# Sparse cross-attention: the scores of a later tile between the two halves of a tile's sums of values, and four columns of negated maxima

## The chip, the cores and the metric

One core of one Trainium2 chip runs the whole program. The metric is the device time in microseconds (us) of one execution; lower is better. TensorE is PE in the profile, VectorE is DVE, ScalarE is ACT, GpSimd is POOL and SyncE is SP. Each engine runs its own instructions strictly in the order in which the program gives them, and waits at semaphores for the others.

## The reference

The program is a four-layer perceiver on `x` [16, 64, 128] with a context of 16 x 1601 x 128. Each layer has a cross-attention, an attention and a feed-forward. The change lies in the cross-attention of the last layer, where each query keeps only its 32 highest of 1601 scores in each of 16 heads:

```python
Q = _split_heads(x @ Wq.T + bq, N_HEADS)
K = _split_heads(knowledge_embeddings @ Wk.T + bk, N_HEADS)
V = _split_heads(knowledge_embeddings @ Wv.T + bv, N_HEADS)
scores = jnp.einsum('bhsd,bhnd->bhsn', Q, K) / SCALE
k = min(TOP_K, N)                                   # 32
topk_scores, topk_indices = jax.lax.top_k(scores, k)
sparse_weights = jax.nn.softmax(topk_scores, axis=-1)
sel_V = jnp.take_along_axis(V[:, :, None, :, :], topk_indices[..., None], axis=3)
context = jnp.einsum('bhsk,bhskd->bhsd', sparse_weights, sel_V)
context = context.transpose(0, 2, 1, 3).reshape(B, S, D_MODEL)
return context @ Wo.T + bo
```

## The kernel before

The stages of the program follow one another. The change is in `topk_cross_attention` alone, which runs from about 2660 us to 4140 us of the span.

Its work is cut into T = 128 tiles. A tile is one batch and two of its 16 heads: 128 rows (2 heads x 64 queries) by 1601 keys. Eight tiles (TB = 8) make a batch. The kernel doesn't gather the 32 chosen values: it makes a dense 128 x 1601 matrix P that is zero outside the chosen scores, and multiplies P by the context. A tile goes through these steps, each named as in the code:

- `scores(t)` on PE (L925): four blocks of keys into psS, the one score buffer of four banks. It waits until `copy_scores(t-1)` and `fold(t-1)` have read the previous tile out of psS.
- `copy_scores(t)` on ACT (L1012): psS to SS, three buffers.
- `fold(t)` on DVE (L1162): the pairwise maxima of the two halves of a row. It reads psS and SS.
- `find` and `drop` on DVE (MAX8 at L1184, MATCH_REPLACE8 at L1193): the 32 highest, eight at a time. `find(t,0)`, `drop(t,0)`, `find(t,1)`, `drop(t,1)` belong to one turn of the loop, `find(t,2)`, `drop(t,2)`, `find(t,3)` to the next. `add_halves` (L1111) and `take_maxes` (L1118) on POOL prepare the pairwise minima for the later ones.
- `negate(t)` on DVE (L1200): the row's maximum times -1 into a column of `mneg`, which has two columns. Before it writes a column it waits for `exps(t-2)`, which read it.
- `exps(t)` on ACT (L1018): EX = exp(SS + mneg).
- `count_sides` (ACT, L1030), `count_above` (DVE, L1211), `count_equal` (three small steps on POOL, L1126 to L1132) and `mark` (ACT, L1039 and L1042) make P, a one for each chosen score; `weigh` on POOL (L1139) multiplies it by EX.
- `turn(t,q)`, q = 0 to 3, on PE (L935) transposes P in four groups of blocks into psT, and `copy_weights(t,q)` on ACT (L1050) copies each to PT. `values(t,q)` on PE (L947) multiplies each group by the context into psU: 4, 4, 4 and 1 products, each two instructions in the trace. So `values(t,0)` and `values(t,1)` are 16 rows, `values(t,2)` and `values(t,3)` are 10.
- `inverse(t)` on DVE (L1218), `norm(t)` on ACT (L1058), `turn_u(t)` on PE (L959) and `copy_ut(t)` on ACT (L1066) scale and transpose the result. After every 16 tiles a pair of batches is summed over the heads in four parts, `sums` (PE, L968) and `add` (DVE, L1225), each in a turn of its own.

Each engine runs one loop over s = 0, 1, 2, ... in which steps of different tiles stand beside one another. In turn s, ACT has: `count_sides(s-2)`, `copy_scores(s+1)`, `norm(s-4)`, `copy_weights(s-3, 0 and 1)`, `mark(s-2)`, `copy_weights(s-3, 2 and 3)`, `exps(s-1)`, `copy_ut(s-4)`. DVE has: `find(s,0)`, `find(s-1,2)`, `negate(s)`, `drop(s,0)`, `drop(s-1,2)`, `find(s,1)`, `inverse(s-4)`, `find(s-1,3)`, `drop(s,1)`, `add` in some turns, `fold(s+1)`, `count_above(s-1)`. POOL has: `take_maxes(s)`, `count_equal(s-2)`, `add_halves(s+1)`, `weigh(s-2)`, and once in eight turns `spread` (L1101), which spreads the next batch's queries. PE's order is the loop at L975, in the listing.

Three kinds of turns differ in length. In a key turn (t = s-3 is one of the first four tiles of a batch, in the first 15 batches) PE also projects a block of the next batch's keys (`project`, L914) and ACT copies it (`keys`, L1005). In a sum turn (28 of them: t mod 16 = 5, 6, 7 or 13, from t = 21 on) stand `sums` and `add`; `turn_u` waits for that `add`. All others are plain turns.

Of the kernel before, what the change touches and what calls it, by code (L numbers as in the profile page):

```python
# [5 lines left out]
ALU = mybir.AluOpType  # L6
ACT = mybir.ActivationFunctionType
# [9 lines left out]
K = 1601  # L17
# [10 lines left out]
ONE = 1  # L28
# [764 lines left out]
def topk_cross_attention(c, N, QT, WkT, bk):  # L793
# [4 lines left out]
    T = B * TB  # L798
# [7 lines left out]
    with ExitStack() as st:  # L806
# [4 lines left out]
        SS = c.sb(st, "SS", [128, 3, KP])  # L811
        maxes = c.sb(st, "maxes", [128, 2, HALF])
        pairs = c.sb(st, "pairs", [128, 3, KP])
        EX = c.sb(st, "EX", [128, 2, K])
        P = c.sb(st, "P", [128, 2, K])
        PT = c.sb(st, "PT", [128, 2, NC, 128])
        top = c.sb(st, "top", [128, 3, TOPK])
        mneg = c.sb(st, "mneg", [128, 2])
        above = c.sb(st, "above", [128, 2])
        below = c.sb(st, "below", [128, 2])  # L820
        sides = c.sb(st, "sides", [128, K])
# [29 lines left out]
        exp_done, marked = c.sem("exp_done"), c.sem("marked")  # L851
# [7 lines left out]
        with nc.Block() as block:  # L859
            @block.gpsimd  # L860
            def _(pool):
                for j in range(2):
                    pool.memset(ctxN[:, j, :, D:D + 1], 1.0).then_inc(filled, 1)
                for j in range(3):
                    pool.memset(SS[:, j, K:KP], LOW).then_inc(filled, 1)
                pool.tensor_tensor(c.x[:], c.x[:], bc(c.bias_row[:].rearrange("p (a d) -> p a d", a=1), [128, NT, D]),
                                   ALU.add).then_inc(filled, 1)
                pool.wait_ge(filled, 6 + ONE)

        with nc.Block() as block:  # L870
# [24 lines left out]
            @block.tensor  # L895
            def _(pe):
                def bank_free(use):
                    u = slot[use]
                    if u >= 2:
                        kind, a, n = uses[u - 2]  # L900
                        if kind == "keys":
                            pe.wait_ge(kt_ready, BLOCKS * a + n + 1 + ONE)
                        else:
                            pe.wait_ge(pt_ready, 4 * a + n + 1 + ONE)
                    return u % 2

                def project(b, n):
                    o, w = KB[n]
                    pe.wait_ge(turned_loaded[b % 2], 16 * (b // 2 + 1) + ONE)
                    if b == 0:  # L910
                        keys = psS[:, o:o + w]
                    else:
                        keys = psT[:, bank_free(("keys", b, n)), 0:w]
                    pe.matmul(keys, WkT, ctxT[:, b % 2, o:o + w], start=True, stop=True).then_inc(kp_ready, 1)  # L914

                def scores(t):
                    b, n = t // TB, t % TB
                    if n == 0:
                        pe.wait_ge(kt_ready, BLOCKS * (b + 1) + ONE)
                        pe.wait_ge(stat_ready, b + 1 + ONE)  # L920
                    if t:
                        pe.wait_ge(copied, t + ONE)
                        pe.wait_ge(folded, t + ONE)
                    for o, w in KB:
                        last = pe.matmul(psS[:, o:o + w], stat[:, b % 2, 2 * n:2 * n + 2, :], KT[:, b % 2, o:o + w],  # L925
                                         start=True, stop=True)
                    last.then_inc(scored, 1)

                def turn(t, q):
                    if q == 0:  # L930
                        pe.wait_ge(p_ready, t + 1 + ONE)
                    j = bank_free(("weights", t, q))
                    for k in range(4 * q, min(4 * q + 4, NC)):
                        o, w = KC[k]
                        last = pe.transpose(psT[0:w, j, (k % 4) * 128:(k % 4) * 128 + 128], P[:, t % 2, o:o + w],  # L935
                                            c.ident[:])
                    last.then_inc(turned, 1)

                def values(t, q):
                    if q == 0:  # L940
                        pe.wait_ge(loaded[t // TB % 2], 32 * (t // TB // 2 + 1) + ONE)
                    if q == 0 and t:
                        pe.wait_ge(us_ready, t + ONE)
                    pe.wait_ge(pt_ready, 4 * t + q + 1 + ONE)
                    for k in range(4 * q, min(4 * q + 4, NC)):
                        w = KC[k][1]
                        last = pe.matmul(psU[:, 0:D + 1], PT[0:w, t % 2, k, :], ctxN[0:w, t // TB % 2, k, 0:D + 1],  # L947
                                         start=(k == 0), stop=(k == NC - 1))
                    if q == 3:
                        last.then_inc(u_ready, 1)  # L950

                def turn_u(t):
                    pe.wait_ge(us_ready, t + 1 + ONE)
                    if t:
                        pe.wait_ge(ut_ready, t + ONE)
                    if t + 1 in summed:
                        p, g = summed[t + 1]
                        pe.wait_ge(y_added, PARTS * p + g + 1 + ONE)
                    pe.transpose(psZ[:, 0:128], U[:, t % 2, :], c.ident[:]).then_inc(u_turned, 1)  # L959

                def sums(p, g, turned_sums):
                    pe.wait_ge(ut_ready, turned_sums + ONE)
                    n = PARTS * p + g
                    if n:
                        pe.wait_ge(y_added, n + ONE)
                    heads = range(g * H // PARTS, (g + 1) * H // PARTS)
                    for h in heads:
                        last = pe.matmul(psZ[:, 128:256], UT[:, p % 2, h, :, :], N[:, h, :], start=(h == heads[0]),  # L968
                                         stop=(h == heads[-1]))
                    last.then_inc(y_ready, 1)  # L970

                for n in range(BLOCKS):
                    project(0, n)
                scores(0)
                for s in range(T + 3):  # L975
                    if s + 1 < T:
                        scores(s + 1)
                    t = s - 3
                    if t in summed:
                        sums(*summed[t], t - 1)  # L980
                    if t in keyed:
                        project(*keyed[t])
                    if t >= 0:
                        turn(t, 0)
                        turn(t, 1)
                    if t >= 1:
                        turn_u(t - 1)
                    if t >= 0:
                        turn(t, 2)
                        turn(t, 3)  # L990
                        for q in range(4):
                            values(t, q)
                turn_u(T - 1)
                for g in range(PARTS):
                    sums(NT - 1, g, T)

            @block.scalar
            def _(act):
# [15 lines left out]
                def exps(t):  # L1014
                    act.wait_ge(max_ready, t + 1 + ONE)
                    if t >= 2:
                        act.wait_ge(p_ready, t - 1 + ONE)
                    act.activation(EX[:, t % 2, :], SS[:, t % 3, 0:K], ACT.Exp, bias=mneg[:, t % 2:t % 2 + 1]  # L1018
                                   ).then_inc(exp_done, 1)

                def count_sides(t):
# [50 lines left out]
                for s in range(T + 3):  # L1072
                    if 0 <= s - 2 < T:
                        count_sides(s - 2)
                    if s + 1 < T:
                        copy_scores(s + 1)
                    if s >= 4:
                        norm(s - 4)
                    if s - 3 in keyed:
                        keys(*keyed[s - 3])  # L1080
                    if s >= 3:
                        copy_weights(s - 3, 0)
                        copy_weights(s - 3, 1)
                    if 0 <= s - 2 < T:
                        mark(s - 2)
                    if s >= 3:
                        copy_weights(s - 3, 2)
                        copy_weights(s - 3, 3)
                    if 0 <= s - 1 < T:
                        exps(s - 1)  # L1090
                    if s >= 4:
                        copy_ut(s - 4)
# [63 lines left out]
            def _(dve):  # L1156
# [38 lines left out]

                def negate(t):
                    dve.wait_ge(listed_early, EARLY * t + 1 + ONE)
                    if t >= 2:
                        dve.wait_ge(exp_done, t - 1 + ONE)
                    dve.tensor_scalar(mneg[:, t % 2:t % 2 + 1], top[:, t % 3, 0:1], -1.0, None, ALU.mult  # L1200
                                      ).then_inc(max_ready, 1)

                def count_above(t):
# [2583 lines left out]
```

## Time and profile before

| what | value |
|---|---|
| time, median of 3 runs | 4362.37 us (4357.18 to 4365.47) |
| time of the profiled execution | 4360.0 us |
| its span | 4358.3 us |
| mean granted clock of TensorE | 0.918 |
| busy: PE, DVE, ACT, POOL | 80%, 75%, 63%, 33% |

The span is the time from the first instruction to the last of the profiled execution; 1.7 us of its time lie outside. Busy shares are of the whole span, over all stages.

### The profile page before, as it was taken

What the parts mean: (1) busy time and instruction counts of PE and PEld (TensorE: products, weight loads), DVE (VectorE), ACT (ScalarE), POOL (GpSimd) and SP (SyncE); (2) the same over time, 40 slices, a digit from 0 to 9 for tenths busy, and PEclk for the clock granted to TensorE, in tenths of its full rate; (3) what the DMA queues carried; (4) which work ended last, traced back from release to release, by engine and by line L of the source; (5) the groups of instructions that cost most, each with busy time, mean ns of one, the idle gap of its engine ahead of it and who ended that gap; (6) DMA issues with size and microseconds to landing.
All of it is one profiled execution on the core that took longest, in us unless ns stands there. A gap on an engine that the chain in (4) does not pass through costs nothing. (4 is left out here: it accounts for less than half of the span.)

```text
span 4358.3 us, 71374 instructions
## 1 busy us (share of the span) xinstructions
PE 3497.7 (80%) x25855; PEld 2833.5 (65%) x25855; DVE 3281.8 (75%) x5582; ACT 2749.1 (63%) x4270; POOL 1438.7 (33%) x1185
## 2 busy tenths in 40 slices
PE   5435749999999788999999885777777777777787
PEld 3334337999999566999999852555555555555676
DVE  4675877777777624877787656999999999999744
ACT  3112616666666444666666533998899988998832
POOL 0000503111210201211121013776776767766510
PEclk9555859999999898999999987999999999999998
DMA  8744011101110121111110001000000000000000
GB/s 274 108 57 110 4 41 39 38 31 39 39 31 16 24 64 36 39 31 31 39 38 24 19 10 41 16 16 16 31 16 16 16 16 31 16 16 8 1 23 19
DMA packets 186346, 161.34 MB, mean 37 GB/s; under 512 B 7996, under 2 KB 174092, under 8 KB 185996
## 3 DMA queue, kind: packets, MB, share of 16 engines
q1 hardware_dynamic: 182604, 142.83, 12.4%
q10 hardware_dynamic: 3392, 13.93, 0.9%
q8 instruction: 208, 3.41, 0.3%
q14 instruction: 142, 1.16, 0.1%
HBM read 127.36 MB, written 20.20 MB: 34 GB/s over the span
## 5 line engine op out<-in xcount | busy, mean ns | idle before, releaser
L559 PEld LDWEIGHTS psU<-ctxN,ST 128*128 128x128 f32 x6656 | 852.5, 191 | 98.4 <-issue 39.7
L559 PE MATMUL psU<-ctxN,ST 128*128 128x129 f32 x6656 | 866.8, 275 | 20.7 <-issue 20.7
L645 ACT ACTIVATE ST<-ST 128x512 f32<-128x512 f32 (+1 forms) x832 | 513.3, 625 | 165.8 <-DVE ST L747 161.6
L1184 DVE MAX8 top<-pairs 128x8 f32<-128x1602 f32 (+1 forms) x384 | 587.6, 1536 | 0.0
L1139 POOL TENSOR_TENSOR P<-P,EX 128x1601 f32<-128x1601 f32 x128 | 459.8, 3592 | 385.3 <-ACT P L1042 385.3
L947 PE MATMUL psU<-ctxN,PT 128*128 128x129 f32 (+1 forms) x3328 | 439.8, 286 | 158.3 <-ACT PT L1050 158.3
L747 DVE TENSOR_TENSOR ST<-ST,psB 128x512 f32<-128x512 f32 (+1 forms) x832 | 556.3, 677 | 2.8 <-PE psB L578 2.7
L733 DVE TENSOR_TENSOR psA<-psA,ST 128x512 f32<-128x512 f32 x640 | 446.6, 698 | 138.0 <-ACT ST L637 70.5
L947 PEld LDWEIGHTS psU<-ctxN,PT 128*128 128x128 f32 (+1 forms) x3328 | 407.7, 199 | 178.4 <-ACT PT L1050 178.4
L547 PE MATMUL psS<-statL,ctxH 128*128 128x512 f32 x832 | 394.3, 474 | 3.9 <-ACT ST L640 1.9
L925 PE MATMUL psS<-KT,stat 128*128 128x512 f32 (+1 forms) x1024 | 378.6, 512 | 16.8 <-DVE maxes L1162 16.0
L677 POOL CAST ctxH<-ctxM 128x1601 fp32r<-128x1601 f32 x30 | 45.6, 1521 | 1012.5 <-DVE ctxM L706 1012.5
L637 ACT ACTIVATE ST<-psS,key_bias 128x512 f32<-128x512 f32 (+1 forms) x416 | 283.9, 682 | 145.6 <-PE psS L547 140.2
L1193 DVE MATCH_REPLACE8 pairs<-top,pairs 128x801 f32<-128x801 f32 (+1 forms) x256 | 357.3, 1396 | 0.0
L640 ACT ACTIVATE ST<-psS 128x512 f32<-128x512 f32 (+1 forms) x416 | 246.5, 592 | 166.9 <-PE psS L547 161.5
L547 PE MATMUL psS<-statH,ctxH 128*128 128x512 f32 x832 | 332.0, 399 | 0.0
L935 PE MATMUL psT<-ident,P 128*128 128x128 f32 (+1 forms) x1664 | 255.6, 283 | 94.3 <-ACT KT L1005 74.0
L547 PE MATMUL psS<-statH,ctxL 128*128 128x512 f32 x832 | 328.9, 395 | 0.0
L925 PEld LDWEIGHTS psS<-KT,stat 128*128 128x128 f32 x1024 | 185.9, 191 | 205.6 <-issue 204.6
L935 PEld LDWEIGHTS psT<-ident,P 128*128 128x128 f32 (+1 forms) x1664 | 194.5, 144 | 157.8 <-ACT KT L1005 88.2
L1012 ACT ACTIVATE SS<-psS 128x1601 f32<-128x1601 f32 x128 | 193.0, 1508 | 137.8 <-PE psS L925 137.8
L1050 ACT ACTIVATE PT<-psT 128x512 f32<-128x512 f32 (+1 forms) x512 | 239.3, 507 | 19.2 <-PE psT L935 19.2
(509 smaller groups left out, 6734.8 us busy)
## 6 DMA issues: line engine op xcount, KB each, us to landing
ctxN<-in_ctx SPq DMA_DIRECT2D x48, 768.0 KB
ahead_ctxT<-ctxT_scratch SPq DMA_DIRECT2D x32, 800.5 KB, 4.3
ctxT_scratch<-trn ACTq DMA_DIRECT2D x16, 800.5 KB
ctxT<-ctxT_scratch SPq DMA_DIRECT2D x16, 800.5 KB, 6.1
nat<-in_ctx SPq DMA_DIRECT2D x16, 768.0 KB
dist_scratch<-dd SPq DMA_DIRECT2D x8, 800.5 KB
skewed<-in_ctx SPq DMA_DIRECT2D x8, 768.0 KB
ctx_late<-in_ctx SPq DMA_DIRECT2D x8, 768.0 KB
```

The lines of the kernel that those rows point to most:

```text
L547: last = pe.matmul(psS[:, i % RING, :], x[:, u // 2 % 2, o:o + 128], q[:, p % 2, heads, queries], start=(n_pass == 0), stop=(n_pass == 2))
L559: last = pe.matmul(psU[:, q, 0:D + 1], ST[0:n, i % SLOTS, q * 128:q * 128 + 128], ctxN[0:n, j, k, 0:D + 1], start=(k == 0 and q % 2 == 0), ...
L637: act.activation(ST[0:n, i % SLOTS, :], psS[0:n, i % RING, :], ACT.Identity, bias=key_bias[0:n, col:col + 1]).then_inc(copied, 1)
L645: act.activation(ST[0:n, i % SLOTS, :], ST[0:n, i % SLOTS, :], ACT.Exp).then_inc(exp_done, 1)
L733: dve.tensor_tensor(psA[:], psA[:], cell, ALU.max).then_inc(folded, 1)
L747: dve.tensor_tensor(cell, cell, psB[0:n, :], ALU.subtract).then_inc(shifted, 1)
L925: last = pe.matmul(psS[:, o:o + w], stat[:, b % 2, 2 * n:2 * n + 2, :], KT[:, b % 2, o:o + w], start=True, stop=True)
L935: last = pe.transpose(psT[0:w, j, (k % 4) * 128:(k % 4) * 128 + 128], P[:, t % 2, o:o + w], c.ident[:])
L947: last = pe.matmul(psU[:, 0:D + 1], PT[0:w, t % 2, k, :], ctxN[0:w, t // TB % 2, k, 0:D + 1], start=(k == 0), stop=(k == NC - 1))
L1139: pool.tensor_tensor(P[:, j, :], P[:, j, :], EX[:, j, :], ALU.mult).then_inc(p_ready, 1)
L1184: dve.max(top_t[:, 8 * n:8 * n + 8], own).then_inc(listed_early if n < 2 else listed_late, 1)
L1193: dve.match_replace(left, top_t[:, 8 * n:8 * n + 8], maxes[:, t % 2, :] if n == 0 else left, LOW).then_inc(listed_early if n < 2 else list ...
```

## The change

`mneg` gets four columns in place of two, so `negate(t)` waits for `exps(t-4)` in place of `exps(t-2)`. On PE, the scores of tile s+2 are issued between `values(t,1)` and `values(t,2)` of turn s (t = s-3), where before the scores of tile s+1 stood at the head of turn s, which is behind `values(t-1,3)`. Two tiles' scores are issued ahead of the loop in place of one. No instruction is added or taken away.

```diff
-        mneg = c.sb(st, "mneg", [128, 2])
+        mneg = c.sb(st, "mneg", [128, 4])
@@ PE
                 scores(0)
+                scores(1)
                 for s in range(T + 3):
-                    if s + 1 < T:
-                        scores(s + 1)
                     t = s - 3
@@ PE
                     if t >= 0:
                         turn(t, 2)
                         turn(t, 3)
-                        for q in range(4):
-                            values(t, q)
+                        values(t, 0)
+                        values(t, 1)
+                    if s + 2 < T:
+                        scores(s + 2)
+                    if t >= 0:
+                        values(t, 2)
+                        values(t, 3)
@@ ACT, exps(t)
-                    act.activation(EX[:, t % 2, :], SS[:, t % 3, 0:K], ACT.Exp, bias=mneg[:, t % 2:t % 2 + 1]
+                    act.activation(EX[:, t % 2, :], SS[:, t % 3, 0:K], ACT.Exp, bias=mneg[:, t % 4:t % 4 + 1]
@@ DVE, negate(t)
-                    if t >= 2:
-                        dve.wait_ge(exp_done, t - 1 + ONE)
-                    dve.tensor_scalar(mneg[:, t % 2:t % 2 + 1], top[:, t % 3, 0:1], -1.0, None, ALU.mult
+                    if t >= 4:
+                        dve.wait_ge(exp_done, t - 3 + ONE)
+                    dve.tensor_scalar(mneg[:, t % 4:t % 4 + 1], top[:, t % 3, 0:1], -1.0, None, ALU.mult
```

PE at the second key turn of the first batch, before. L925 is the scores, L914 the key block, L935 the transposes of P, L959 the transpose of the result, L947 the values:

```order
L947 MATMUL psU<-ctxN,PT 128x129 x13
L925 MATMUL psS<-KT,stat 128x512 x3
L925 MATMUL psS<-KT,stat 128x65
L914 MATMUL psT<-ctxT,WT 128x512
L935 MATMUL psT<-ident,P 128x128 x8
L959 MATMUL psZ<-ident,U 128x128
L935 MATMUL psT<-ident,P 128x128 x4
L935 MATMUL psT<-ident,P 65x128
L947 MATMUL psU<-ctxN,PT 128x129 x13
L925 MATMUL psS<-KT,stat 128x512 x3
```

The same place after:

```order
L947 MATMUL psU<-ctxN,PT 128x129 x5
L914 MATMUL psT<-ctxT,WT 128x512
L935 MATMUL psT<-ident,P 128x128 x8
L959 MATMUL psZ<-ident,U 128x128
L935 MATMUL psT<-ident,P 128x128 x4
L935 MATMUL psT<-ident,P 65x128
L947 MATMUL psU<-ctxN,PT 128x129 x8
L925 MATMUL psS<-KT,stat 128x512 x3
L925 MATMUL psS<-KT,stat 128x65
L947 MATMUL psU<-ctxN,PT 128x129 x5
```

The 13 products of a tile are now 8 and 5 with the scores between them, and the next turn's work follows the last five directly.

PE at a sum turn, where L968 is a part of the sum over the heads, before:

```order
L947 MATMUL psU<-ctxN,PT 128x129 x13
L925 MATMUL psS<-KT,stat 128x512 x3
L925 MATMUL psS<-KT,stat 128x65
L968 MATMUL psZ<-N_261,UT 128x128 x4
L935 MATMUL psT<-ident,P 128x128 x8
L959 MATMUL psZ<-ident,U 128x128
```

And after:

```order
L947 MATMUL psU<-ctxN,PT 128x129 x8
L925 MATMUL psS<-KT,stat 128x512 x3
L925 MATMUL psS<-KT,stat 128x65
L947 MATMUL psU<-ctxN,PT 128x129 x5
L968 MATMUL psZ<-N_261,UT 128x128 x4
L935 MATMUL psT<-ident,P 128x128 x8
L959 MATMUL psZ<-ident,U 128x128
```

The part of the sum and the transposes now stand behind the last five products, no longer behind the scores. The orders of ACT, DVE and POOL are unchanged.

## Rows read from the trace of the kernel before

**Rows 1.** The page: busy time and share of the span of each engine.

```profile
PE 3497.7 (80%) x25855; PEld 2833.5 (65%) x25855; DVE 3281.8 (75%) x5582; ACT 2749.1 (63%) x4270; POOL 1438.7 (33%) x1185
```

**Rows 2.** Waits, 3000 to 3800 us: waiting <- releaser: total us, times, longest.

```profile
DVE mneg L1200 <- ACT EX L1018: 70.1, 71, 2.2
ACT SS L1012 <- PE psS L925: 67.5, 71, 2.7
...
PE psZ L959 <- DVE x L1225: 37.7, 17, 2.7
```

**Rows 3.** Line L1012, the copies of scores: shortest/median/longest ns, first and last start.

```profile
L1012 ACT ACTIVATE SS<-psS x128: 1504/1507/1517, 2671.0 to 4094.1; 128x1601 f32<-128x1601 f32 x128
```

**Rows 4.** Timeline, ACT, start of the stage: start, duration us [idle before <-releaser].

```profile
2704.50 1.51 ACT L1012 ACTIVATE SS<-psS 128x1601 f32<-128x1601 f32 x1 [2.35 <-PE psS L925]
```

**Rows 5.** Windows, plain and key turn: us; busy PE, PEld, DVE, ACT, POOL; PEclk.

```profile
3415.52:3426.22 10.70, 7.95 (x49) 5.82 (x48) 10.25 (x16) 9.91 (x12) 7.78 (x7) 1.00 0.12 32
3426.22:3437.87 11.65, 8.80 (x51) 6.16 (x51) 10.26 (x16) 10.59 (x13) 9.36 (x8) 1.00 0.35 114
```

**Rows 6.** Timeline, all engines, one plain turn and its neighbours.

```profile
3410.90 3.58 POOL L1139 TENSOR_TENSOR P<-P,EX 128x1601 f32<-128x1601 f32 x1 [2.75 <-ACT P L1042]
...
3413.09 0.15 DVE L1200 TENSOR_SCALAR mneg<-top 128x1 f32<-128x1 f32 x1 [1.66 <-ACT EX L1018]
...
3414.44 1.90 POOL L1118 TENSOR_TENSOR pairs<-pairs,maxes 128x801 int32<-128x801 int32 x1
...
3415.52 1.51 ACT L1012 ACTIVATE SS<-psS 128x1601 f32<-128x1601 f32 x1 [0.77 <-PE psS L925]
...
3416.82 0.15 DVE L1218 RECIPROCAL li<-psU 128x1 f32<-128x1 f32 x1
...
3417.00 0.37 ACT L1058 ACTIVATE U<-psU,li 128x128 f32<-128x128 f32 x1
3417.01 0.29 POOL L1132 TENSOR_SCALAR rest<-span,above 128x1 f32<-128x1 f32 x1
...
3418.22 1.64 ACT L1039 ACTIVATE P<-sides,rest 128x1601 f32<-128x1601 f32 x1
...
3418.56 1.96 PE L947 MATMUL psU<-ctxN,PT 128*128 128x129 f32 x16
...
3419.57 0.98 DVE L1162 TENSOR_TENSOR maxes<-psS,SS 128x801 f32<-128x801 f32 x1
...
3421.43 0.73 ACT L1050 ACTIVATE PT<-psT 128x512 f32<-128x512 f32 x2
...
3421.60 3.59 POOL L1139 TENSOR_TENSOR P<-P,EX 128x1601 f32<-128x1601 f32 x1 [2.74 <-ACT P L1042]
...
3422.06 1.38 PE L947 MATMUL psU<-ctxN,PT 128*128 128x129 f32 x10 [1.54 <-ACT PT L1050]
3422.07 1.62 ACT L1018 ACTIVATE EX<-SS,mneg 128x1601 f32<-128x1601 f32 x1
...
3423.28 2.91 PE L925 MATMUL psS<-KT,stat 128*128 128x512 f32 x8
...
3423.79 0.15 DVE L1200 TENSOR_SCALAR mneg<-top 128x1 f32<-128x1 f32 x1 [0.45 <-ACT EX L1018]
...
3426.22 1.51 ACT L1012 ACTIVATE SS<-psS 128x1601 f32<-128x1601 f32 x1 [0.76 <-PE psS L925]
```

**Rows 7.** Timeline, a batch's first key turn, and the copy four turns on.

```profile
3427.01 1.61 POOL L1118 TENSOR_TENSOR pairs<-pairs,maxes 128x801 int32<-128x801 int32 x1
...
3429.30 0.29 POOL L1132 TENSOR_SCALAR rest<-span,above 128x1 f32<-128x1 f32 x1
...
3429.89 1.62 ACT L1039 ACTIVATE P<-sides,rest 128x1601 f32<-128x1601 f32 x1
...
3472.47 1.51 ACT L1012 ACTIVATE SS<-psS 128x1601 f32<-128x1601 f32 x1 [0.77 <-PE psS L925]
```

**Rows 8.** Timeline, PE, the wait in a sum turn.

```profile
3487.64 0.30 PE L959 MATMUL psZ<-ident,U 128*128 128x128 f32 x1 [2.68 <-DVE x L1225]
```

## Prediction, made before the changed kernel ran

> **What bounds the kernel now.** I read the page first: over the span PE is busy 80%, DVE 75%, ACT 63% [rows 1], an average over ten stages that says nothing of this one. The stage runs tiles one after another, and its pace can be read at one instruction per tile, the copy of the scores. The first of the 128 copies starts at 2671.0 and the last at 4094.1 [rows 3]: 1423.1 us for 127 turns, 11.21 on average. A plain turn, from the copy at 3415.52 to that at 3426.22, takes 10.70, and no engine fills it: PE 7.95, POOL 7.78, ACT 9.91, DVE 10.25 [rows 5]. So a loop of waits sets the pace, and the view of waits names candidates: in 71 turns ACT waited 67.5 us for the scores, and DVE's negation waited 70.1 us for the exponential [rows 2]. The timeline of the plain turn shows both as closed loops:
>
> Loop 1, through PE's order. From the copy (3415.52) ACT works without a gap until the later copies of weights (3421.43): 5.91. PE's last five products start at 3422.06: 0.63. The scores behind them start at 3423.28: 1.22. The next copy starts at 3426.22: 2.94. Sum 10.70 [rows 6].
>
> Loop 2, through the two columns. Negate (3413.09) to norm (3417.00), with DVE's reciprocal ending at 3416.97 just ahead of it: 3.91. Norm to the exponential (3422.07): 5.07. The exponential: 1.62. On to the next negate (3423.79): 0.10. Sum 10.70 [rows 6].
>
> Both loops have the length of the turn. Opening one of them alone should therefore do nothing in a plain turn. The reader is to see that the listed wait is small (0.76 at the copy, 0.45 at the negate [rows 6]) while the loop behind it is the whole turn.
>
> **The change part by part.**
>
> *Scores ahead (loop 1).* No instruction comes or goes. The scores for the copy that starts norm minus 1.48 of the next turn are now issued behind the first 16 value rows of this one. Those run 3418.56 to 3420.52; the scores overlap a predecessor by 0.16 as they do at 3423.28 (the products before end at 3423.44), so they start 3.36 behind norm (3417.00) and end 2.91 later, at norm + 6.27. The copy wants them at norm + 8.45 (a turn of 9.93, below). ACT's 0.77 goes, with 2.2 to spare. The scores also need the fold of the tile before, which now stands in front of the last value rows too: it runs 3419.57 to 3420.55 [rows 6], as late as the place itself, so at today's phase it costs nothing or 0.1. The last ten value rows slip from 3422.06 to norm + 6.1 and end at norm + 7.5. Who waits for those? DVE's reciprocal of the next turn, at norm + 9.75, and the transposes, which need POOL's product (3421.60 + 3.59, norm + 8.2). Both come later, so the slip is hidden.
>
> *Four columns (loop 2).* Negate then waits for an exponential two turns older, which is long done. DVE is free to run at its own work, 10.25 per plain turn [rows 5].
>
> *What is late next.* ACT's own work. Plain turn: 10.70 - 0.77 = 9.93. Key turns: the four between the copies at 3426.22 and 3472.47 take 46.25, each with an idle 0.77 at its copy, so 46.25 - 3.08 = 43.17 for four [rows 6, 7]. DVE's 10.25 lies above 9.93 but below the 10.79 of a key turn, and over eight turns ACT needs 43.17 + 39.72 = 82.9 against DVE's 82.0. DVE is tied to ACT at two points only: its reciprocal must be ready for norm, and its fold must follow the copy. Fold starts 2.60 behind the end of the reciprocal (3416.97 to 3419.57), so DVE may run up to 2.6 ahead, or 2.3 when it meets the slipped value rows. It gains 0.5 per key turn and loses 0.32 per plain turn, so the store holds for a batch: 2.2 gained, 1.3 lost, and up to 0.6 more for the additions (0.2 in each of up to three sum turns). I take ACT as the pace, and keep DVE's price for the rivals.
>
> *POOL.* Product (3410.90) to maxima (3414.44), 3.54; on to the end of the last small step (3417.30), 2.86; then mark, 3418.22 to the next product at 3421.60, 3.38 [rows 6]. With a semaphore's 0.03 that is 9.81, still under 9.93. Once per batch `spread` stands in it: product 3421.60 to the end of the small steps 3429.59 is 7.99, and mark began at 3429.89 [rows 6, 7], 12.89 behind norm (3417.00). With the turn shorter by 0.77 mark wants to start at norm + 12.12, while POOL is ready at norm + 12.62, or 0.27 later where maxima take 1.90 instead of 1.61. Stall 0.5 to 0.8; I take 0.7, 15 times. Bounds: 0 (POOL was early) to 1.0.
>
> *Sum turns.* `turn_u` waits for the addition, 2.68 [rows 8]; in the old order this pushed the values and so the scores. After, the scores have 2.2 to spare, and DVE being ahead shortens the wait itself. So I price them as plain turns, 9.93; bound above: the addition's 0.2 in each of 27.
>
> *Start and end.* Up to the copy at 2704.50 the stage waits for DVE's folds, in the same order as before: 33.55 unchanged [rows 3, 4]. The drain behind the last copy has no copies of scores: unchanged.
>
> **The sum.** 127 intervals: 4 at the start, 60 of key turns (15 batches), 63 others. 33.55 + 15 x 43.17 + 63 x 9.93 + 15 x 0.7 = 33.55 + 647.6 + 625.6 + 10.5 = 1317.2. Before, 1423.1. Saved 105.9 us, against the profiled execution's 4360.0: 4254.1. That execution lies 2.4 below the median, so I forecast 4256, its own range 4246 (no stall of mark) to 4268.
>
> **Rivals.**
>
> *DVE sets the plain turns.* For: it is the fullest engine at 10.25, and its lead may not build up. Against: the store above. Price: 63 x (10.25 - 9.93) + 27 x 0.2 = 26; time 4282.
>
> *POOL sets them.* Against: its loop is 9.81. For: it is 0.12 from the bound, and the same maxima step takes 1.90 at 3414.44 and 1.61 at 3427.01 [rows 6, 7]. If every turn bore another 0.29, the loop would be 10.10: 63 x 0.17 + 15 x 0.3 = 15; time 4271. The Trainium skill (SBUF — State Buffer, "Who interferes with whom") says that a DVE instruction with two SBUF inputs and a GpSimd one that reads SBUF exclude each other for a whole instruction; by that rule a DVE without gaps would hit POOL more often. DVE's long instructions here (MAX8, MATCH_REPLACE8) list one large SBUF input or a pair of which one is a short list, and the products measured 3.58 and 3.59 [rows 6], so the trace doesn't show such a lock.
>
> *A third loop of the old length.* Two loops of 10.70 are a warning that there might be more. Then plain turns stay at 10.70 and only key and sum turns gain: 63 x 0.77 = 48.5 less saved; time 4304. Against: every other loop I followed is 9.81 or less.
>
> *Slower.* The scores now stand in front of the last value rows and wait for the fold. That closes a loop on PE and DVE: fold 0.98, scores 2.91, values 1.38, reciprocal some 0.1 later, and from its start at 3416.82 to the next fold at 3419.57, 2.75 [rows 6]. Sum 8.1. It decides only above 9.93 and costs time against before only above 11.21, so it must grow by 3.1. PE at half its clock would do that: 4.29 more, 12.4 per turn, 127 x 1.2 = 152, time 4514. The granted clock is 1.00 in both turns [rows 5], and PE's idle time per plain turn shrinks from 2.75 to 1.98. The Trainium skill (TensorE: Matmul & The Clock Gate, "What's actually happening") says that TensorE's default is the throttled level and that activity releases it; by that rule the shorter idle time speaks for a full clock, and gives this rival little.
>
> *Nothing happens.* If the copy already waited for something else than the order of PE (the fold, say), moving the scores would do nothing: 4362. Against: before the scores PE ran without a gap from 3422.06 [rows 6].
>
> **How the numbers follow.** Forecast 0.72, DVE 0.10, POOL 0.06, third loop 0.06, no change 0.02, slower 0.04. A difference of 0.2% (9 us) is about what a measurement of this kernel can tell from none. Faster by more: 0.72 + 0.10 + 0.06 + 0.06 = 0.94; same 0.02; slower 0.04. The range goes from 4246, where mark never stalls, to 4286, above DVE's case. It leaves out the last three cases (0.12) and some 0.07 of the first.
>
> **What would show it.** In the profile after: plain turns of 9.9 to 10.0 and key turns of 10.8 at the copies; no idle time at the copy of the scores for PE; no wait of negate for the exponential; a short wait of mark (L1039) for POOL's small steps in the first key turn of a batch; DVE's new idle time at the fold (for the copy) or the reciprocal (for the values). Plain turns of 10.25 with norm waiting for the reciprocal would show the DVE case; mark waiting in every plain turn, the POOL case; 10.70, a third loop. The forecast is wrong if DVE's lead is kept from building up by a wait I haven't seen, or if ACT's own work grows once it runs without a gap.

## The result, and the profile after

The changed kernel takes 4255.89 us (median of 4 runs, 4251.12 to 4259.73) against 4359.77 us (4 runs, 4356.76 to 4365.47). The ratio is 0.976, with a 95% interval of 0.9742 to 0.9777. The forecast was 4256 us. The profiled execution took 4252.25 us, its span 4250.5.

Line L1016, the copies of scores (L1012 before), which answers to [rows 3]:

```profile
L1016 ACT ACTIVATE SS<-psS x128: 1504/1507/1518, 2667.9 to 3987.2; 128x1601 f32<-128x1601 f32 x128
```

From the first copy to the last it is 1319.3 us, 103.8 less than before; the forecast was 1317.2. The rest of the program, which the change doesn't touch, came out 4.0 shorter (2931.2 against 2935.2 of the two spans).

The timeline of a plain turn after, all engines, answers to [rows 6] (start, duration us):

```profile
3413.25 1.51 ACT L1016 ACTIVATE SS<-psS 128x1601 f32<-128x1601 f32 x1
...
3414.65 0.36 ACT L1062 ACTIVATE U<-psU,li 128x128 f32<-128x128 f32 x1
...
3414.95 0.99 DVE L1166 TENSOR_TENSOR maxes<-psS,SS 128x801 f32<-128x801 f32 x1
...
3416.20 1.96 PE L947 MATMUL psU<-ctxN,PT 128*128 128x129 f32 x16
...
3418.00 2.91 PE L925 MATMUL psS<-KT,stat 128*128 128x512 f32 x8
...
3418.65 0.14 DVE L1204 TENSOR_SCALAR mneg<-top 128x1 f32<-128x1 f32 x1
...
3420.75 1.33 PE L947 MATMUL psU<-ctxN,PT 128*128 128x129 f32 x10
...
3422.36 0.15 DVE L1222 RECIPROCAL li<-psU 128x1 f32<-128x1 f32 x1
...
3423.18 1.51 ACT L1016 ACTIVATE SS<-psS 128x1601 f32<-128x1601 f32 x1
...
3424.58 0.36 ACT L1062 ACTIVATE U<-psU,li 128x128 f32<-128x128 f32 x1
```

The turn is 9.93 (3413.25 to 3423.18), without a wait at the copy or at the negation. The scores start 3.35 behind norm (3.36 were worked out) and end 2.3 before the next copy. DVE's reciprocal ends 2.07 before the norm that needs it (3422.51 to 3424.58): this is DVE's lead, 0.03 before (3416.97 to 3417.00 in [rows 6]).

Waits of the changed kernel, 3000 to 3800 us, which answer to [rows 2] (waiting <- releaser: us in total, times, longest):

```profile
PE psT L935 <- ACT KT L1009: 59.5, 37, 2.0
...
PE psZ L959 <- DVE x L1229: 41.3, 20, 2.8
...
DVE li L1222 <- PE psU L947: 15.1, 18, 2.3
...
ACT P L1043 <- POOL rest L1136: 5.1, 8, 0.7
```

The rows in which negate waited for the exponential and ACT for the scores are gone. ACT waits up to 0.7 for POOL at mark, 8 times, in the first key turn of a batch. New is DVE's wait for the values at its reciprocal.

### The profile page after: what moved, and what is told of

It is laid out like the page before. It is cut to its first block and busy times, and to the rows that moved or that the text cites. A ratio compares the mean times of both kernels' runs of the same rounds, so it can differ in the third digit from the quotient of the medians.

```text
span 4250.5 us, 71372 instructions
## 1 busy us (share of the span) xinstructions
PE 3506.3 (82%) x25855; PEld 2847.3 (67%) x25855; DVE 3271.4 (77%) x5582; ACT 2742.5 (65%) x4270; POOL 1437.4 (34%) x1185
## 5 line engine op out<-in xcount | busy, mean ns | idle before, releaser
L733 DVE TENSOR_TENSOR psA<-psA,ST 128x512 f32<-128x512 f32 x640 | 446.2, 697 | 137.4 <-ACT ST L637 69.5
L947 PE MATMUL psU<-ctxN,PT 128*128 128x129 f32 (+1 forms) x3328 | 454.3, 291 | 3.3 <-ACT PT L1054 3.3
L947 PEld LDWEIGHTS psU<-ctxN,PT 128*128 128x128 f32 (+1 forms) x3328 | 427.0, 206 | 3.8 <-ACT PT L1054 3.8
L925 PE MATMUL psS<-KT,stat 128*128 128x512 f32 (+1 forms) x1024 | 379.4, 513 | 17.4 <-DVE maxes L1166 16.4
L935 PE MATMUL psT<-ident,P 128*128 128x128 f32 (+1 forms) x1664 | 265.6, 291 | 143.4 <-ACT KT L1009 94.2
L935 PEld LDWEIGHTS psT<-ident,P 128*128 128x128 f32 (+1 forms) x1664 | 193.5, 144 | 219.0 <-ACT KT L1009 108.4
L925 PEld LDWEIGHTS psS<-KT,stat 128*128 128x128 f32 x1024 | 186.9, 193 | 206.8 <-issue 205.3
L1122 POOL TENSOR_TENSOR pairs<-pairs,maxes 128x801 int32<-128x801 int32 x128 | 229.7, 1794 | 2.3 <-DVE maxes L1166 2.1
```

The source lines that it names most:

```text
L733: dve.tensor_tensor(psA[:], psA[:], cell, ALU.max).then_inc(folded, 1)
```

## The experiments

The runs were made in three sittings, each beside the kernel before, so ratios to it are compared: the changed kernel has 0.976. Where a gain of few us is at stake, I go by the sum of the 127 intervals between the copies in the profiled execution: the rest of the program, the same in all these kernels, took 2931.2 to 2943.5 us in their profiled executions, and the times carry that. The sum is 1423.1 before and 1319.3 after; it is one execution of each.

### e1: the scores alone

```diff
-        mneg = c.sb(st, "mneg", [128, 4])
+        mneg = c.sb(st, "mneg", [128, 2])
-                    if t >= 4:
-                        dve.wait_ge(exp_done, t - 3 + ONE)
+                    if t >= 2:
+                        dve.wait_ge(exp_done, t - 1 + ONE)
```

(The column indices in `exps` and `negate` go back to `t % 2` too.)

> The scores of tile s+2 stand between the value rows as in the changed kernel, but the negated maxima keep two columns. Theory A (two loops of the same length, 10.70 us in a plain turn and 11.65 in a key turn, each of which alone holds the pace): the loop through the two columns stays, so plain turns stay at 10.7 and key turns at 11.65, ACT's idle 0.77 moves from the copy of the scores to norm (which waits for DVE's reciprocal), and only what the sum turns lost through PE's order comes back: before, the 127 intervals summed to 1423.1, against 33.55 + 15 x 46.25 + 63 x 10.70 = 1401.4, so about 22 us. Time 4338 (4330 to 4348). Rival B (the two waits are separate costs that add): the 0.77 at each of 123 copies goes, 95 us: 4265.

Measured: 4375.42 us, ratio 1.0015 (1.0006 to 1.0024); intervals 1438.6. Plain turns stay at 10.70 (but for seven of 9.93, each right behind a sum turn of 12.2, and two single ones) and most key turns at 11.65, so the loop through the columns holds the pace alone, as theory A has it, and rival B is out. But the 22 us of the sum turns didn't come back: the intervals grew by 15, with sum turns up to 13.5. The timeline of e1, one sum turn:

```profile
3126.14 1.51 ACT L1016 ACTIVATE SS<-psS 128x1601 f32<-128x1601 f32 x1
...
3128.30 0.37 ACT L1062 ACTIVATE U<-psU,li 128x128 f32<-128x128 f32 x1 [0.65 <-DVE li L1222]
...
3131.29 0.45 PE L959 MATMUL psZ<-ident,U 128*128 128x128 f32 x1 [4.07 <-DVE x L1229]
...
3132.60 3.65 PE L947 MATMUL psU<-ctxN,PT 128*128 128x129 f32 x16
...
3139.63 1.51 ACT L1016 ACTIVATE SS<-psS 128x1601 f32<-128x1601 f32 x1 [2.87 <-PE psS L925]
```

And the windows of e1, the plain turn before it and this turn (us; busy PE, PEld, DVE, ACT, POOL; granted clock; DMA share, GB/s):

```profile
3115.43:3126.14 10.71, 8.59 (x56) 6.50 (x55) 10.27 (x16) 9.93 (x13) 7.80 (x7) 1.00 0.01 2
3126.14:3139.63 13.49, 9.42 (x42) 7.42 (x42) 12.51 (x18) 9.94 (x13) 9.78 (x10) 0.75 0.00 1
```

PE is done with the scores early and then stands 4.07 us before `turn_u`, which waits for DVE's addition. Behind that gap the granted clock is at the lower of its two levels (1.2 and 2.4 GHz) for a while (0.75 of full speed over the turn), and 16 rows of values take 3.65 us, not 1.96. The scores stand behind them, so the copy comes 2.87 late.

The gap and the clock can be told apart. In the sum turn of e1 from 3773.56 the same gap lasts 4.08, the granted clock is 0.86, and the turn takes 12.21. And these are windows of the kernel before, two sum turns in each of which PE stood 2.68 before `turn_u`:

```profile
3121.18:3133.82 12.64, 9.96 (x58) 8.31 (x58) 12.39 (x20) 9.90 (x13) 9.13 (x10) 0.86 0.00 1
3144.44:3155.44 11.00, 8.32 (x57) 6.66 (x57) 10.75 (x17) 9.90 (x12) 8.08 (x7) 1.00 0.11 32
```

Against a plain turn's 10.70, 0.30 goes with the gap and 1.64 more with the slower clock. Eleven of the 27 sum turns before take 12.3 to 12.6 in this way, some 17 of the 22 us that sum turns lost. The two turns of [rows 5] show nothing of it.

### e2: the four columns alone

```diff
@@ before.py: four columns, scores in their old place
-                    if t >= 2:
-                        dve.wait_ge(exp_done, t - 1 + ONE)
+                    if t >= 4:
+                        dve.wait_ge(exp_done, t - 3 + ONE)
```

(The width and the column indices of `mneg` are those of the change.)

> Four columns of negated maxima, the scores in their old place at the head of the turn. Theory A (two loops of the same length): PE's order still holds plain turns at 10.70 and key turns at 11.65; the idle time at the copy of the scores stays at 0.77. DVE runs ahead of ACT and so does the addition of a sum turn earlier, which shortens the wait of turn_u (2.68 before) and brings back most of the 22 us that sum turns lost: 4340 (4335 to 4362). Rival B (separate costs): negate's wait, 70.1 us in 71 turns, goes: 4240 to 4265.

Measured: 4328.88 us, ratio 0.9917 (0.990 to 0.9933); intervals 1391.9. Timeline of e2, a plain turn:

```profile
3403.64 1.51 ACT L1012 ACTIVATE SS<-psS 128x1601 f32<-128x1601 f32 x1 [0.77 <-PE psS L925]
...
3405.04 0.36 ACT L1058 ACTIVATE U<-psU,li 128x128 f32<-128x128 f32 x1
...
3405.18 0.99 DVE L1162 TENSOR_TENSOR maxes<-psS,SS 128x801 f32<-128x801 f32 x1 [0.36 <-ACT SS L1012]
...
3414.25 1.51 ACT L1012 ACTIVATE SS<-psS 128x1601 f32<-128x1601 f32 x1 [0.77 <-PE psS L925]
```

The idle 0.77 at the copy stays and the turn is 10.61, so again one open loop doesn't free a plain turn. Sum turns are now plain turns (10.62), because DVE runs ahead (its fold waits for the copy) and its addition is there in time; that is the 22 us that were forecast. The other 9 are a correction: copy to norm takes 1.40 here, 1.48 before (3415.52 to 3417.00 in [rows 6]). In the kernel before, norm was held back 0.08 by the reciprocal, and no row lists so small a wait. PE's loop alone is 10.62, and only that of the columns 10.70.

### e3: the scores one place earlier

```diff
                         turn(t, 3)
+                    if s + 2 < T:
+                        scores(s + 2)
+                    if t >= 0:
                         values(t, 0)
                         values(t, 1)
-                    if s + 2 < T:
-                        scores(s + 2)
```

> As the changed kernel, but the scores of tile s+2 stand before all four groups of values instead of between the second and third. The scores then want to start 1.56 us behind norm instead of 3.36, where the fold that they wait for ends between 1.3 (DVE 2.3 ahead of ACT) and 3.6 (DVE not ahead). Theory A (ACT's own work is the pace, and PE has room): a turn in which DVE is not ahead closes the loop fold 0.98, scores 2.91, all values 3.2, reciprocal 0.1, to the next fold 2.75, which is 9.95, about the 9.93 of a plain turn, and 1.0 more in a key turn is still under 10.79 by little: 0 to 15 us slower than the changed kernel, 4256 to 4271. Rival C (the place in the middle matters because the wait for the fold blocks PE): ACT stalls at norm for the reciprocal in most turns, 0.5 or more each: 4320 or slower.

Measured: 4268.09 us, ratio 0.9775 (0.976 to 0.979); intervals 1324.7. So 5 us slower than the changed kernel by the intervals, within theory A's range (the ratios don't resolve it); rival C is out. The wait of the scores for the fold shows (25.9 us in 25 turns between 3000 and 3800), and nearly all of it is covered.

### e4: one more ACT instruction per turn

```diff
                     if s >= 4:
                         copy_ut(s - 4)
+                    act.activation(spare[:, s:s + 1], c.eps[:], ACT.Copy)
```

> As the changed kernel, with one more ACT instruction in each turn: a copy of one column into a column that nothing reads, behind copy_ut. Such an instruction measured 202 ns by itself and costs some 0.15 us between neighbours. Theory A (ACT's own work is the pace everywhere): 131 turns x 0.15 = 20 us slower than the changed kernel: 4276 (4268 to 4284). Rival D (DVE sets the plain turns, or POOL does): only the 60 key turns grow, 9 us; plain turns stay as they are: 4265 or less.

Measured: 4270.73 us, ratio 0.978 (0.9766 to 0.9795); intervals 1329.6. Plain turns go from 9.93 to 10.03 and key turns from 10.88 to 10.98: the instruction costs 0.10 there, not the 0.15 of the estimate, and the intervals grow by 10, not 20. By that sum alone rival D (9 us) couldn't be told from this; the plain turns decide, which it would have left alone. ACT's own work is the pace of both kinds.

### e5: POOL's spread ahead of the product

```diff
+                    if s % TB == 2 and s // TB + 1 < B:
+                        spread(s // TB + 1)
                     if s >= 2:
                         weigh(s - 2)
-                    if s % TB == 2 and s // TB + 1 < B:
-                        spread(s // TB + 1)
```

> As the changed kernel, with POOL's spread of the next batch's queries in front of the product instead of behind it. There POOL idles 1.94 to 1.97 us per plain turn, and spread takes 1.9. Theory A (mark waits 0.5 to 0.8 in the first key turn of each batch because spread delays POOL's small steps): that wait goes, the first key turn falls from 11.4 or 11.7 to 10.9: 15 x 0.7 = 10 us faster than the changed kernel: 4246 (4243 to 4252). Rival E (the wait is due to something else in that turn, or spread now delays the product by as much): 4256.

Measured: 4257.04 us, ratio 0.9756 (0.9741 to 0.9771); intervals 1316.1. The wait goes as forecast: the first key turn falls from 11.4 or 11.7 to 10.88, 9.8 us in 14 batches. But by the intervals only 3 us are left of it, because sum turns of every second batch grow to 10.5 and 10.8. The timeline of e5, one such turn and the copy that ends it:

```profile
3090.94 0.16 DVE L1222 RECIPROCAL li<-psU 128x1 f32<-128x1 f32 x1
...
3091.87 0.36 ACT L1062 ACTIVATE U<-psU,li 128x128 f32<-128x128 f32 x1
...
3094.12 0.44 PE L959 MATMUL psZ<-ident,U 128*128 128x128 f32 x1 [2.83 <-DVE x L1229]
...
3095.42 2.80 PE L947 MATMUL psU<-ctxN,PT 128*128 128x129 f32 x16
...
3101.00 1.51 ACT L1016 ACTIVATE SS<-psS 128x1601 f32<-128x1601 f32 x1 [0.68 <-PE psS L925]
```

And two turns on, a sum turn that takes 9.93:

```profile
3111.79 1.51 ACT L1016 ACTIVATE SS<-psS 128x1601 f32<-128x1601 f32 x1
3112.55 0.15 DVE L1222 RECIPROCAL li<-psU 128x1 f32<-128x1 f32 x1
3113.19 0.36 ACT L1062 ACTIVATE U<-psU,li 128x128 f32<-128x128 f32 x1
...
3115.72 0.30 PE L959 MATMUL psZ<-ident,U 128*128 128x128 f32 x1 [2.03 <-DVE x L1229]
```

The 0.7 that ACT waited for POOL was time in which DVE built up its lead. Without it the lead is 0.77 at the norm of the first timeline, 0.06 a turn later and 0.49 in the second one. With so small a lead the addition comes late and PE stands 2.83 before `turn_u`. The granted clock of that turn is 0.84, 16 rows take 2.80, and ACT waits 0.68 for the scores: it is e1's chain again. DVE's own work is not the pace there; DVE itself then waits 0.79 for the values (at 3102.17). That an earlier addition alone ends such turns, with no work taken from DVE, e9 and e12 show below.

### e6, e7 and e8: the copy of the key block first, with spread, and with the additional instruction

```diff
+                    if s - 3 in keyed:
+                        keys(*keyed[s - 3])
                     if s + 1 < T:
                         copy_scores(s + 1)
                     if s >= 4:
                         norm(s - 4)
-                    if s - 3 in keyed:
-                        keys(*keyed[s - 3])
```

e7 is this with e5's edit, and e8 is e7 with e4's edit.

> As the changed kernel, with ACT's copy of the key block in front of the copy of the scores instead of behind norm. PE projects the block right behind the last value rows, so it is there by then. Theory A: the transposes of the second group no longer wait for that copy behind the first group's, and the idle 0.26 us at the second copy of weights in a key turn goes: 60 x 0.26 = 16 us at most. ACT would need 81.9 us for eight turns, and DVE needs 82.0 with the additions in 27 turns more, so DVE takes over as the pace and some of it is lost: 5 to 16 us faster than the changed kernel, 4240 to 4251. Rival F (the copy of the key block now waits for PE, which finishes the value rows late): no gain or a loss, 4256 to 4265.

> Both moves: spread in front of the product, and the copy of the key block in front of the copy of the scores. Theory A (ACT and DVE now bound the stage together, DVE with 10.25 us a turn): the two gains of 10 and up to 16 us don't add in full: 4232 to 4244. ACT's own work alone would give 4230; DVE's, 33.5 + 123 x 10.2 + 27 x 0.2 = 1293.5 against 1319.3 measured, also 4230. If they add in full and more, down to 4225, DVE's share was priced too high.

> Both moves and the additional ACT instruction of e4. Theory A (DVE is now the pace as much as ACT): the additional instruction costs less than its full 20 us, some 5 to 15: 4240 to 4255. If it costs the full amount that it costs in e4, ACT is still the only pace after both moves, and DVE's lead carries it.

Measured: e6 4233.67 us, ratio 0.9701 (0.9686 to 0.9715), intervals 1292.4. e7 4235.85 us, 0.9706 (0.9692 to 0.9721), 1299.1. e8 4233.66 us, 0.9702 (0.9686 to 0.9718), 1292.5. e6 gained 27 by the intervals where at most 16 were expected: the last key turn fell from 10.51 to 9.93 and two others from 10.88 to 10.31, 0.57 each and not 0.26. The two copies of weights take 0.95 together where they took 1.36 (their start to the start of mark), which is 0.41, and the copy of the key block starts 0.19 sooner behind `count_sides` than the copy of the scores did. The gains of e5 and e6 don't add, and the additional instruction, 10 us in e4, costs nothing in e8, whose time lies below the 4240 to 4255 that were expected; e8 is even 6.5 us under e7, the kernel that it adds to. The windows of 2680 to 3960 us, in order the changed kernel, e6 and e8:

```profile
2680.00:3960.00 1280.00, 1046.60 (x6130) 781.16 (x6129) 1251.70 (x1859) 1232.21 (x1514) 964.22 (x747) 0.96 0.06 18
```

```profile
2680.00:3960.00 1280.00, 1062.55 (x6242) 773.45 (x6243) 1277.54 (x1899) 1240.15 (x1540) 983.88 (x761) 0.98 0.06 18
```

```profile
2680.00:3960.00 1280.00, 1059.57 (x6228) 767.49 (x6227) 1277.02 (x1899) 1248.59 (x1662) 983.02 (x760) 0.98 0.06 18
```

DVE (third) is busy 1277.5 and 1277.0 of 1280: its own work is now the pace. e7 is the exception, with 1270.4 of the same 1280: in three early sum turns (12.09, 12.14, 11.26) PE stood 3.1 to 3.4 before `turn_u` and ACT waited up to 2.3 for the scores, as in e1.

### e9, e10, e11 and e12: the addition of a sum turn right behind the reciprocal

```diff
                     if s >= 4:
                         inverse(s - 4)
+                    if s - 3 in summed:
+                        add(*summed[s - 3])
                     if late:
                         find(s - 1, 3)
                     if early:
                         drop(s, 1)
-                    if s - 3 in summed:
-                        add(*summed[s - 3])
```

e9 is the changed kernel with this edit; e10 is e1 with it, e11 is e6 with it, and e12 is e7 with it.

> As the changed kernel, with DVE's addition in a sum turn right behind the reciprocal instead of behind the fourth MATCH_REPLACE8, 2.7 us earlier. turn_u then waits 0 to 0.5 us instead of 2.0. Theory A (the changed kernel hides that wait behind the 2.2 us that the scores have to spare, except in the last sum turns, where DVE's lead is used up and turns of 10.65 and 10.78 show): 0 to 4 us faster than the changed kernel, 4252 to 4256. Rival G (the wait costs something in each sum turn): 27 x 0.4 or more, 4245 or less.

> As e1 (scores ahead, two columns), with the addition right behind the reciprocal. In e1 turn_u waited 4.07 us in a sum turn, the granted clock of that turn was 0.75, 16 rows of values took 3.65 instead of 1.96, and the scores came 2.87 late: turns of 13.5. Theory A (PE's gap at turn_u and the slower clock behind it are what sum turns lose in e1): with the gap gone, all sum turns fall to 10.7, the 127 intervals from 1438.6 to 1401 (33.5 + 15 x 46.25 + 63 x 10.70), the time to 4338 (4333 to 4345), granted clock 0.98 again. Rival H (sum turns lose because PE's sum stands behind the last value rows, or by the clock alone for another reason): still 4355 or more.

> Copy of the key block ahead (e6) and the addition ahead. In e6 ACT waits 1.1 to 1.5 us for the key block's product in the first key turn behind the batch's last sum turn, since PE came late from turn_u's 2.0 wait for the addition. Theory A: in the seven batches that end in sum turns this goes, 7 x 1.2 = 8 us faster than e6: 4225 (4218 to 4231). If DVE's own work is the pace in e6 (an additional ACT instruction cost nothing there), the gain is smaller: 4228 to 4234.

> e11 with spread in front of the product as well. Theory A (spread's delay of mark is a wait of ACT in which DVE catches up, so taking it away only helps where DVE isn't the pace): the same as e11 within 4 us. Rival E (independent gains): 10 us faster than e11.

Measured: e9 4259.48 us, ratio 0.976 (0.9745 to 0.9775), intervals 1316.6. The turns of 10.65 and 10.78 at the end of the stage are 9.93, and the other sum turns are 9.93 as before, so the changed kernel does hide the wait elsewhere. The other 1 us came off key turns, one of 11.34 and several of 10.6 to 10.8. The times don't resolve 3 us, and the median came out above the range I gave.

e10 4344.92 us, ratio 0.9957 (0.994 to 0.9974), intervals 1405.2. From e1's 1438.6 this is 33 less by one move that takes away no work: all 27 sum turns are 10.70. Waits of e10, 3000 to 3800 us:

```profile
DVE mneg L1204 <- ACT EX L1022: 62.5, 72, 1.9
...
PE psZ L959 <- ACT U L1062: 52.9, 36, 1.8
ACT U L1062 <- DVE li L1222: 46.7, 71, 1.0
```

No wait of `turn_u` for the addition is left. So the gap at `turn_u`, with the slower clock behind it, is what e1's sum turns lost. A few key and plain turns still show 11.0 to 12.1, and the granted clock of the stage (2680 to 4060 us) is 0.93, not the 0.98 that I expected; PE still waits up to 2.8 for the copy of the key block. The loop of the columns is in the waits as it should be: negate for the exponential, norm for the reciprocal.

e11 4229.64 us, ratio 0.9693 (0.9679 to 0.9708), intervals 1292.1; e12 4233.67 us, 0.9699 (0.9685 to 0.9714), 1292.4. They and e6 can't be told apart. All three beat both kernels: 3.0% to 3.1% under the kernel before, 0.6% to 0.7% under the changed one by the ratios. All three end at 1292, and so does e8, though ACT waits at different places: in e6 once a batch 1.1 to 1.45 for the key block's product, in e11 once a batch 0.95 to 1.3 for POOL at mark, in e12 scattered, mostly under 0.5. DVE is busy 1277.5, 1277.3 and 1276.6 of the 1280 us, so 1292 is what it needs. e12 also has none of e7's long sum turns.

## Why the prediction was right, and where it wasn't

The mechanism was right; that 4256 met the median to 0.1 us is luck. The intervals came out 2.1 longer than worked out, the rest of the program 4.0 shorter without a cause in the change, and inside the 9.93 of a plain turn two errors of about 10 us each over the stage cancel.

*Two loops of one length.* Right: e1 leaves plain turns at 10.70 and e2 at 10.62, and only both edits together give 9.93. The size was off by 0.08: PE's loop was 10.62, and a wait of norm too short to be listed made it look like 10.70.

*ACT's own work is late next.* Right: plain turns of 9.93, key turns of 10.88, 10.88 and 10.51, and e4 showed that ACT's work sets both. The 9.93 was reached by two errors that cancel. Norm's hidden 0.08 should have come off too. And taking the listed 0.77 off as a whole was 0.09 too much: less that wait the copy would start 1.71 behind the start of `count_sides` (in e2, 3411.77 to 3414.25 less 0.77), but without a wait it starts 1.80 behind it (3411.45 to 3413.25).

*POOL's spread.* Right in place and size. The timeline of the changed kernel, the first key turn of a batch:

```profile
2955.56 1.63 ACT L1043 ACTIVATE P<-sides,rest 128x1601 f32<-128x1601 f32 x1 [0.68 <-POOL rest L1136]
```

The excess of the first key turns over 10.88 was 0.80 or 0.52, 0.70 on average, as taken. What I didn't see is that this wait is also DVE's chance to get ahead (e5).

*DVE's lead.* Right for the batches. From the reciprocals and the norms of all 128 tiles the lead mostly tops out at 2.3, falls by 0.22 per plain turn (0.32 was worked out) and by 0.42 per sum turn, and is back at the top in a batch or two. So DVE's own work is 10.15 per plain turn, not the 10.25 read from [rows 5]. In the last tile of five batches the lead was down to 0.04 to 0.07, and no plain or sum turn of those batches grew. It failed where no key turns follow: the last seven intervals sum to 71.5, not 69.5. Windows of the changed kernel, a sum turn in which PE stood 2.74 before `turn_u`, and one of the last seven, in which it stood 2.83:

```profile
3674.13:3684.07 9.94, 7.20 (x48) 5.56 (x47) 9.94 (x17) 9.82 (x13) 7.80 (x7) 1.00 0.01 2
3925.63:3936.28 10.65, 7.83 (x40) 6.17 (x39) 10.65 (x17) 9.82 (x12) 8.52 (x7) 0.84 0.01 2
```

The first is hidden, the second, with the slower clock, isn't; the copy that ends it waits 0.80 for the scores, and the turn behind takes 10.78. These two turns are 1.6 of the 2.0, and e9 shows that the late addition makes them. Only the last two intervals (10.13 and 10.15, the lead at 0.03) are DVE's own pace. The 2.0 are the size of the 2.1 by which 1317.2 was short; the rest (the start of the stage 1.2 shorter, the 14 batches 1.3 longer) cancels.

*Sum turns as plain turns.* Right: 9.93 in all but two of the last ones, with 1.5 to 2.8 us of wait at `turn_u` hidden. What such a wait can cost I saw only in e1: there it has grown to 4.07, and a turn loses up to 2.8. That the sum turns before lost most of their 22 us with the slower clock stands nowhere in the prediction.

*PE's clock.* This step was wrong, in a rival. I argued from PE's idle time per turn, which shrinks, that the clock would stay. But the granted clock of the stage fell from 0.98 (2680 to 4060 us) to 0.96 (2680 to 3960). In the kernel before, the first key turn of [rows 7] has this wait:

```profile
3428.71 0.66 PE L935 MATMUL psT<-ident,P 128*128 128x128 f32 x4 [1.17 <-ACT KT L1005]
```

Timeline of the changed kernel, second key turn of the same batch as above:

```profile
2965.26 0.66 PE L935 MATMUL psT<-ident,P 128*128 128x128 f32 x4 [2.02 <-ACT KT L1009]
...
2966.88 3.46 PE L947 MATMUL psU<-ctxN,PT 128*128 128x129 f32 x16
...
2974.30 0.17 DVE L1222 RECIPROCAL li<-psU 128x1 f32<-128x1 f32 x1 [2.29 <-PE psU L947]
```

Its windows, with the granted clock ahead of the last two columns:

```profile
2965.00:2968.00 3.00, 2.59 (x16) 2.36 (x17) 3.00 (x5) 2.74 (x4) 1.62 (x2) 0.77 0.00 0
2968.00:2971.00 3.00, 3.00 (x14) 2.56 (x14) 3.00 (x6) 2.97 (x5) 1.18 (x1) 0.66 0.00 0
2971.00:2974.00 3.00, 3.00 (x17) 1.99 (x16) 1.02 (x2) 2.92 (x5) 3.00 (x2) 1.00 0.00 0
```

PE now reaches the second transposes early and waits 2.02 for the copy of the key block, where it waited 1.17 before, in the second key turn too. Behind that the clock falls and 16 rows take 3.46, and DVE waits 2.29 for them. Here DVE pays out of its lead, which drops from 2.35 to 0.68; ACT hardly notices (the last key turn of such batches is 10.52 to 10.79 in place of 10.51). I had looked at the sum of the idle time and at two turns with a clock of 1.00, and not at the single gaps, of which some grew.

*The rivals.* DVE as the pace is not this kernel but e6's; the third loop and "nothing happens" are out by e1 and e2. POOL sets no plain turn: it waits 1.97 for mark in the turn shown above (before its product at 3419.24), no wait of ACT for it is listed in a plain turn, and e4 made plain turns longer by ACT's work alone.

## What to carry to other kernels

Where two waits of a pipelined loop both close loops as long as the turn, open both or expect little: alone, one gave 0.8%, most of it in the sum turns, and the other nothing (ratio 1.0015); together they gave 2.4%. Work out the next bound from the fullest engine's time per turn, add it up over kinds of turns that differ, and look at how far an engine may run ahead: its lead pays for single late results, and a stall that is removed elsewhere may only have been filling that lead. When work on PE is issued earlier, look at where PE will then stand and wait in one piece.

## What the runs showed of the hardware

TensorE's granted clock fell behind single gaps of 2.0 (to 0.77 and 0.66 in the next two windows of 3 us) and 4.07 us (0.75 over a turn of 13.49) in a stage where PE is busy over 80%, and the same 16 rows of values then took 3.46 and 3.65 us instead of 1.96. Other gaps of 2.0 us and more had no such effect (in e5 the one of 2.03 before 3115.72: the granted clock is 1.00 over that turn, and the 16 rows behind it take 1.95; in the changed kernel the one of 2.74 before 3677.68, likewise 1.00 and 1.95). In the kernel before, gaps of 2.68 were followed by a full clock in one turn (1.00) and by a slower one in another (0.86). So the length of the gap alone doesn't tell.

`take_maxes` lasts 1.6 us in every third tile and 1.9 in the other two, in all fourteen profiled executions. The pattern follows the three buffers of `pairs`; why, the runs don't say.
